# Values as weights in the attention's second product, with row sums from the exponential and heads that need no turning

## What is computed

```python
scores = einsum('bsghd,btgd->bghst', q, k) * scale
p = softmax(scores, axis=-1)
out = einsum('bghst,btgd->bsghd', p, v)
...
cat = concatenate([core, xout], axis=-1)
catq = div_clamp_fp8(cat, proj_smooth)       # a scale for each head feature
y = einsum('bsi,oi->bso', catq, wproj) * (proj_in_scale * proj_w_scale)
```

## Time and profile before

| | |
|---|---|
| median of 3 runs | 1736.24 us (1735.25 to 1736.79) |
| the profiled execution | 1738.57 us, its span 1736.7 us |
| TensorE | busy 1632.1 us, 94% of the span |
| VectorE | 1410.2 us, 81% |
| ScalarE | 1359.8 us, 78% |
| GpSimd | 1089.6 us, 63% |
| DMA queue of SyncE | 68.1% of 16 engines' span |
| mean granted TensorE clock | 0.992 |

### The profile page before, as it was taken

How to read it: one execution, slowest core, us unless ns; L and a number is a source line. 1 busy time by engine, 2 the same in 40 slices (tenths; PEclk the granted TensorE clock), 3 DMA queues, 4 the chain that set the end, 5 groups by cost and what they waited for, 6 DMA issues and landing times.

```text
span 1736.7 us, 43799 instructions
## 1 busy us (share of the span) xinstructions
PE 1632.1 (94%) x15491; PEld 1228.0 (71%) x15776; DVE 1410.2 (81%) x3228; ACT 1359.8 (78%) x2908; POOL 1089.6 (63%) x1031
## 2 busy tenths in 40 slices
PE   1569999999999999999999999999999899999999
PEld 1447778888888888888888888888888544444444
DVE  8999999999999999999999999998779763323232
ACT  6978999999999999999999999999999622222221
POOL 1357777777787777777777777778777613121211
PEclk9969999999999999999999999999999999999999
DMA  5947788887888888788878887888999980303000
GB/s 177 223 111 127 140 154 144 148 153 147 148 149 156 147 145 152 147 148 146 151 147 149 148 159 147 145 140 151 188 187 187 196 244 22 138 8 142 4 24 25
DMA packets 663603, 241.45 MB, mean 139 GB/s; under 512 B 619488, under 2 KB 636000, under 8 KB 662880
## 3 DMA queue, kind: packets, MB, share of 16 engines
q1 hardware_dynamic: 662096, 230.20, 68.1%
q0 software_dynamic: 1296, 8.52, 2.4%
HBM read 75.15 MB, written 29.51 MB: 60 GB/s over the span
## 4 chain that ended last, share of the span: by engine, by line
PE 71%; DVE 9%; ACT 7%; issue 5%; POOL 4%; SPq 3%; DMA 2%; DVEq 0%; ACTq 0%; POOLq 0%
PE ps_pj L673 21%; PE ps_s L739 6%; PE ps_o L722 5%; PE ps_o L724 5%; PE ps_o L723 5%; PE ps_s L742 5%; PE ps_s L680 4%; PE ps_qt L692 4%; POOL local L1131 2%; PE ps_s L738 2%; PE ps_pj L811 2%; PE ps_s L825 2%; PE ps_o L811 2%; PE ps_pj L812 2%; PE ps_o L812 2%
## 5 line engine op out<-in xcount | busy, mean ns | idle before, releaser
L1131 POOL TENSOR_TENSOR local<-local 128x512 bf16<-128x512 f32 x512 | 597.1, 1166 | 296.3 <-ACT local L1035 296.0
L673 PE MATMUL ps_pj<-wide 128*128 128x256 bf16 (+1 forms) x5544 | 582.7, 254 | 4.8 <-DVE wide L1214 4.0
L673 PEld LDWEIGHTS ps_pj<-wide 128*128 128x128 bf16 x5544 | 470.1, 98 | 115.0 <-DVE wide L1214 4.4
L1032 ACT ACTIVATE local<-ps_s,neg_max 128x512 f32<-128x512 f32 x512 | 391.8, 765 | 43.7 <-DVE neg_max L1429 41.6
L1035 ACT ACTIVATE local<-ps_s,neg_max 128x512 bf16<-128x512 f32 x512 | 394.0, 770 | 0.0
L722 PE MATMUL ps_o<-v_hi,local 128*128 128x129 bf16 x2048 | 375.5, 221 | 5.7 <-DVE local L1437 3.2
L724 PE MATMUL ps_o<-v_hi,local 128*128 128x129 bf16 x2048 | 375.2, 219 | 0.0
L723 PE MATMUL ps_o<-local 128*128 128x128 bf16 x2048 | 375.1, 218 | 0.0
L1429 DVE TENSOR_REDUCE neg_max<-ps_s 128x1 f32<-128x512 f32 x512 | 344.7, 673 | 22.8 <-PE ps_s L742 22.7
L941 ACT ACTIVATE local<-ps_pj,head_rstd 128x128 f32<-128x128 f32 x756 | 242.0, 448 | 41.8 <-issue 41.7
L1106 POOL TENSOR_TENSOR head_rstd<-sq_sum,minus_half 128x3 f32<-128x3 f32 x256 | 223.4, 873 | 16.4 <-DVE sq_sum L1321 16.4
(11 more groups left out here) (133 smaller groups left out, 2623.5 us busy)
## 6 DMA issues: line engine op xcount, KB each, us to landing
quantised_heads<-local SPq DMA_DIRECT2D x128, 128.0 KB, 2.4
w_raw<-w_group SPq DMA_DIRECT2D x56, 256.0 KB, 3.2
wide<-quantised_heads SPq DMA_DIRECT2D x3, 4096.0 KB, 13.1
local<-local SPq DMA_TRANSPOSE x640, 3.2
wide<-packed_weights SPq DMA_DIRECT2D x32, 256.0 KB, 3.2
wide<-x SPq DMA_DIRECT2D x6, 1024.0 KB, 12.0
packed_weights<-w_proj POOLq DMA_DIRECT2D x4, 1024.0 KB, 15.2
wide<-quantised_heads SPq DMA_DIRECT2D x16, 256.0 KB, 3.4
```

What stands on the lines that cost most here:

```text
L673: last = mm(dst[:, at:at + n], lhs, w_at(par, part, c, cross * 512 + at, n), start=(k == 0), stop=(k == len(terms) - 1))
L1032: a(p_exp[:, u % 2], ps_s[u % 2][:], ACT.Exp, bias=neg_max[:, u % 4:u % 4 + 1])
L1131: tt_(pp[:, u % PP_BUFS, 1], p_exp[:, u % 2], pp[:, u % PP_BUFS, 0], ALU.subtract)\
```

## The change

The value product is turned round: the values are the weights, and P, already transposed, is the moving operand. Two units are taken together, so that a matmul has 256 columns, and twelve matmuls serve two units, six of them at lag 5 of the pair's second unit and six at lag 6. The product comes out with features on partitions. So the heads need no DMA transpose, and a head's smoothing scale is a column, one number for a partition. The row sums no longer come from a column of ones: the first exponential of a unit (L1032) gives its row's sum as an accumulator output. Their reciprocal, 128x4 for a head, goes to DRAM and comes back broadcast to all partitions, 2 KB for each. One y step of 128x512 serves a head and stands in front of the quantiser, whose lags go from 6 and 9 to 8 and 11. ScalarE still writes the high part of the values. The transposes of P now wait for the pair that had the buffer.

```diff
-        PV_LAG, Y_LAG, HEAD_LAG, STORE_LAG = 5, 6, 10, 12
+        PV_LAG, STORE_LAG = 5, 12
+        SUM_LAG, SUM_OUT_LAG, SUM_IN_LAG = 2, 3, 5
-        QUANT_LAG, QUANT_END_LAG = 6, 9
+        QUANT_LAG, QUANT_END_LAG = 8, 11
...
-                            sp.wait_ge(pv_done, SLOTS * g + u - PT_BUFS + 1)
+                            sp.wait_ge(pv_done, SLOTS // 2 * g + (u - PT_BUFS) // 2 + 1)
...
-                    for H in head_at(slot, HEAD_LAG, first):
+                    for H in head_at(slot, SUM_OUT_LAG, first):
+                        n = GROUP_HEADS * g + H
+                        sp.wait_ge(rsum_done, n + 1)
+                        sp.dma_start(sums_dram[n].rearrange("(p t) -> p t", t=TT), r_inv[:, H % 2]).then_inc(sums_out[H % 2], 16)
+                    for H in head_at(slot, SUM_IN_LAG, first):
+                        n = GROUP_HEADS * g + H
+                        sp.wait_ge(sums_out[H % 2], 16 * (n // 2 + 1))
+                        sp.wait_ge(y_done, n - 1 + HEAD_FREE)
+                        sp.dma_start(inv_sums[:, H % 2], sums_dram[n].partition_broadcast(P)).then_inc(sums_in[H % 2], 16)
...
-                        sp.dma_start_transpose(heads_t[:, H % HEADS].rearrange("p (q s) -> p q s", s=P), heads_n[:, H % 2])\
-                            .then_inc(turned[H % 2], 16)
...
-                        sp.dma_start(dst, heads_t[:, h]).then_inc(heads_stored, 16)
+                        sp.dma_start(dst, heads_n[:, H % 2]).then_inc(heads_stored, 16)
...
+            def values(u, start, end):
+
+                b, cross = u // UNITS, u // TT % HEADS // HPG
+                at = (u - 1) % TT * P
+                acc = ps_o[u // TT % 2][:, at:at + 2 * P]
+                pair = slice((u - 1) % PT_BUFS, (u - 1) % PT_BUFS + 2)
+                for tc in range(start, end):
+                    vh, vl = v_hi[:, b % 2, cross, tc], v_lo[:, b % 2, cross, tc]
+                    ph, pl = pt[:, pair, tc], pt[:, pair, TT + tc]
+                    mm(acc, vh, ph, start=(tc == 0), stop=False)
+                    mm(acc, vl, ph, start=False, stop=False)
+                    last = mm(acc, vh, pl, start=False, stop=(tc == TT - 1))
+                return last
...
+                    for u in unit_at(slot, PV_LAG + 1, first):
+                        if u % 2 == 1:
+                            values(u, TT // 2, TT).then_inc(pv_done, 1)
                     for u in unit_at(slot, PV_LAG, first):
...
+                        if u % 2 == 1:
+                            for i in (u - 1, u):
+                                pe.wait_ge(pt_landed[i % PT_BUFS], 16 * SLOTS // PT_BUFS * g + 16 * (i // PT_BUFS + 1))
+                            pe.wait_ge(y_done, GROUP_HEADS * g + u // TT - 1 + HEAD_FREE)
+                            values(u, 0, TT // 2)
...
-                        a(p_exp[:, u % 2], ps_s[u % 2][:], ACT.Exp, bias=neg_max[:, u % 4:u % 4 + 1])
+                        a(p_exp[:, u % 2], ps_s[u % 2][:], ACT.Exp, bias=neg_max[:, u % 4:u % 4 + 1],
+                          accum_out=r_sum[:, H % 2, qt:qt + 1])
...
-                    for u in unit_at(slot, Y_LAG, first):
-                        dve.wait_ge(pv_done, SLOTS * g + u + 1)
-                        v.reciprocal(r_sum[:, u % 4:u % 4 + 1], ps_o[u % 2][:, D:D + 1]).then_inc(rsum_done, 1)
...
-                        v.scalar_tensor_tensor(y[:, H % 2, qt * D:(qt + 1) * D], ps_o[u % 2][:, 0:D],
...
+                    for H in head_at(slot, SUM_LAG, first):
...
+                        v.reciprocal(r_inv[:, H % 2], r_sum[:, H % 2]).then_inc(rsum_done, 1)
...
                     for H in head_at(slot, QUANT_LAG, first):
...
+                        dve.wait_ge(pv_done, 2 * (n + 1))
+                        dve.wait_ge(sums_in[H % 2], 16 * (n // 2 + 1))
+                        v.scalar_tensor_tensor(y[:, H % 2].rearrange("p (t q) -> p t q", q=P),
+                                               ps_o[H % 2].rearrange("p (t q) -> p t q", q=P), smooth_of(g, H),
+                                               inv_sums[:, H % 2].rearrange("p (q t) -> p t q", t=TT), ALU.mult, ALU.mult)\
+                            .then_inc(y_done, 1)
```

More of the change, by code:

```diff
@@ L280, in block_kernel @@
         rsum_done = sem("rsum_done")
+        sums_out = [sem(f"sums_out{i}") for i in range(2)]
+        sums_in = [sem(f"sums_in{i}") for i in range(2)]
         plo_done = sem("plo_done")
         pt_landed = [sem(f"pt_landed{i}") for i in range(PT_BUFS)]
-        turned = [sem(f"turned{i}") for i in range(2)]
         pv_done = sem("pv_done")
@@ L439, in quad_place, with smooth_of @@
             return (q // 2 + 1) % 2, q % 2
-        def smooth_rows_of(group_index, head):
-            return rsmooth[:, bass.ds((group_index % 2) * (HEADS * D) + head * D, D)]
+        def smooth_of(g, H):
+            at = (g + H // GROUP_HEADS) * HEADS + H % HEADS
+            return inv_smooth[:, at:at + 1]
         def tile_bank(i, t):
@@ L581, in group @@
                         load_next_heads(slot - NEXT_HEADS)
[L582 to L585, removed]
-                    for H in head_at(slot, HEAD_LAG, first):
-                        sp.wait_ge(heads_done, GROUP_HEADS * g + H + 1)
[L588 to L591, removed]
-                        sp.dma_start_transpose(heads_t[:, H % HEADS].rearrange("p (q s) -> p q s", s=P), heads_n[:, H % 2])\
-                            .then_inc(turned[H % 2], 16)
-                    for H in head_at(slot, STORE_LAG, first):
-                        sp.wait_ge(turned[H % 2], 16 * GROUP_HEADS // 2 * g + 16 * (H // 2 + 1))
+                    for H in head_at(slot, SUM_OUT_LAG, first):
[7 more added lines that the diff above has]
+                        sp.dma_start(inv_sums[:, H % 2], sums_dram[n].partition_broadcast(P)).then_inc(sums_in[H % 2], 16)
+                    for H in head_at(slot, STORE_LAG, first):
+                        sp.wait_ge(heads_done, GROUP_HEADS * g + H + 1)
                         sp.wait_ge(heads_stored, 16 * (GROUP_HEADS * g + H + FREE))
@@ L1031, in group @@
                             act.wait_ge(plo_done, SLOTS * g + u - 1)
-                        a(p_exp[:, u % 2], ps_s[u % 2][:], ACT.Exp, bias=neg_max[:, u % 4:u % 4 + 1])
+                        H, qt = u // TT, u % TT
+                        if qt == 0 and (not first or H >= 2):
+                            act.wait_ge(rsum_done, GROUP_HEADS * g + H - 1)
+                        a(p_exp[:, u % 2], ps_s[u % 2][:], ACT.Exp, bias=neg_max[:, u % 4:u % 4 + 1],
+                          accum_out=r_sum[:, H % 2, qt:qt + 1])
                         if not first or u >= PP_BUFS:
@@ L1155, in _ @@
             v.reciprocal(rscale, c_("in_scale", 0, SETS * CH)).then_inc(ones_set, 1)
-            v.reciprocal(inv_smooth[:], c_("smooth", 0, G * HEADS)).then_inc(smooth_inverted, 1)
+            v.reciprocal(inv_smooth[:], c_("smooth", 0, G * HEADS))
             v.tensor_tensor(pscale[:], c_("proj_in"), c_("proj_w"), ALU.mult)
@@ L1430, in group @@
                             .then_inc(max_done, 1)
[L1431 to L1440 removed]
+                    for H in head_at(slot, SUM_LAG, first):
+                        n = GROUP_HEADS * g + H
+                        dve.wait_ge(exp_done, TT * (n + 1))
+                        if n >= 2:
+                            dve.wait_ge(sums_out[H % 2], 16 * (n // 2))
+                        v.reciprocal(r_inv[:, H % 2], r_sum[:, H % 2]).then_inc(rsum_done, 1)
                     for n, at in enumerate(CTX_SLOTS if first else ()):
```

55 lines of the change are left out of this document (14 added, 41 removed).

## The result

The changed kernel takes 1887.15 us in the median of 4 runs (1886.15 to 1887.59), the kernel before 1735.74 us beside it (1733.53 to 1736.79): a ratio of 1.0874, 95% interval 1.086 to 1.0887, or 151 us. The forecast was 1749 us, with a range up to 1782. The profiled execution after has 1887.02 us and a span of 1885.2 us.

What follows compares the result with a forecast made beforehand. TensorE was taken to set the pace, VectorE and ScalarE about 5% behind. Terms -13.4 + 29 - 3 + 0 = +12.6 us, put on the timed median of 1736.2, gave 1749 us; 8-in-10 range 1718 to 1782.

Steps and rivals of the forecast that it cites:

- the place: VectorE: the quantiser's new slots meet weight preparation, delaying the maximum; 1.2 us per 16 slots, +29 us, bounds 0 to 72.
- The other three quarters: VectorE, heads without the weight cast: two slots' work sums to 4.83 us, not late, charged nothing.
- the forecast's own limit of 7.0 us: VectorE, cast's quarter, slots 2 and 3 modulo 4: below about 7.0 us the lateness is absorbed; 7.58 forecast.
- y, priced 0.60: VectorE's 128x512 y, priced as the quantiser's last step: 0.60 us, up to twice that for the strided read.
- The read-out, taken at 0.055 us: ScalarE, first exponential's row sum: an instruction's fixed part, 0.055 us a unit, upper bound 0.32.
- the slack that was to take it: ScalarE: 2.28 us needed a slot, averaged over eight, 0.20 us slack; 2.34 with the read-out against 2.46.
- Rival (b): ScalarE: dear read-out, slower from about 0.15 us; 1762 us at 0.20, 1816 at 0.32; chance 0.18.
- TensorE's 13.4 us: Value matmuls: twelve of 256 columns replace twenty-four, saving 0.026 us a slot, 13.4 us over 512 slots.
- Rival (a): TensorE's gain comes through because the late maximum is absorbed: 1722 us, 1712 to 1723 at best; chance 0.28.
- The queue, charged nothing: SyncE's queue and DMAs: moved traffic about equal, transpose landings hidden with 2.3 us left; charged nothing.
- Start and end, taken as -3: VectorE's relief in group 0, worth up to 10 us, taken as -3; after 1340 us 0, bounds -3 and +3.
- full pace in 1060 to 1340 us: Sign that the forecast is right: no slowdown in that stretch, where no weights are prepared.

Runs made afterwards that it cites:

- before_readout: The kernel before with only the first exponential's row sum added, into a tile that nobody reads; 1776.49 us, ratio 1.0239.
- prep_moved: The changed kernel with the weight preparation two slots later, except in the first group; 1791.12 us, ratio 1.0323.
- six_prep_moved: The changed kernel with six buffers for the turned P, y's sums read in order, and weight preparation two slots later; 1782.38 us, ratio 1.0271.
- no_readout: The changed kernel without the first exponential's row sum (sums set to 1 once); 1893.90 us, ratio 1.0911.
- six_bare: six_both without the row sums and without the sums' store and load; 1759.72 us, ratio 1.0139.
- six_both: The changed kernel with six buffers for the turned P, quantiser at lags 6 and 9, sums loaded a slot earlier and read in order; 1803.56 us, ratio 1.0392.
- y_contiguous: The changed kernel with y reading the broadcast sums in order instead of with a step of four elements; 1846.98 us, ratio 1.0637.
- six_swapped: six_both with y running over PSUM and its output in steps, so only the sums are read in order; 1998.82 us, ratio 1.152.
- turned_store: six_both with the sums stored turned, element by element, so y can read them in order; 2520.9 us, ratio 1.451.

## Why the prediction was wrong

The sum of the 151 us, step by step from the kernel before to the changed one: the read-out 41 (before_readout), the rest 15 (prep_moved less before_readout), the place 96 (changed kernel less prep_moved). These are differences along one path, and another order would share them out otherwise: the place's term holds what the strided y and the read-out make of the pile-up, and alone in the kernel before it is 48.

**The step that failed: "The other three quarters have lighter pieces; without any they are ... 4.83, not late, and I charge them nothing."** The mechanism was right and its sign named: VectorE late, maximum late, exponential late, TensorE idle before the scores. But each of the four heads in 16 slots meets a piece of the preparation, and a bare sum was used for three of them. Between the maximum that starts at 802.08 us and the one at 810.53 VectorE is busy 7.86 us (2 x 0.59 maximum, 0.60 end, 1.06 and 1.36 scale pieces, 0.67 tile, 1.17 y, 1.80 quantiser make 7.84) and idle 0.59. The same stretch of the cast's head is 8.03, for which the forecast had 7.58; of the head with the other scale pieces (to 844.26) 8.12; of the head with the weight sums (to 832.91) 6.81. Three heads of four are past the forecast's own limit of 7.0 us where it counted one, and even the fourth is late, after VectorE has waited 1.57 us there for ScalarE's squares. The weights are prepared in this way beside 96 heads (24 times 16 slots), so the 96 us are 1.0 a head, where 1.2 per 16 slots were charged, 0.3 a head. The place alone in the kernel before, 48 us, also lies above the 29. Had I charged each of the three heads by the forecast's own formula (the excess over the limit and 0.6), it would have come to some 75 us with y at 0.60 and to some 115 us with the measured y: estimates from the sums above, on both sides of the 96.

**y, priced 0.60**, takes 1.17 by the starts, just inside the upper bound of 1.2. Of the difference, 0.39 is the strided read (1.133 against 0.739), worth 40 us in the changed kernel (0.31 a head) and 9 us where the pile-up is gone (prep_moved to six_prep_moved, two buffers more included). VectorE's forecast relief of 0.64 us a head was so about 0.1.

**The read-out, taken at 0.055 us**, takes 0.09: inside the bounds and nearer the lower one. What failed is the slack that was to take it: "ScalarE then needs 2.34 us of a slot that TensorE would make 2.46". That is a mean over eight slots, and by the earlier trace rows seven of them were full before: with a turn 2 x 0.57 + 1.33 = 2.47, with a tile 1.14 + 1.28 = 2.42. The free time lay in the one slot with neither. With 0.09 the two kinds need 2.56 and 2.51 us; before_readout shows 2.55 and 2.52. That the slot without turn or tile can't win it back because the next norm waits for GpSimd (0.70 us at 819.17) fits these rows, but no run took that wait away. Rival (b) named this bound and put its start at 0.15 us; at 0.09 it was already passed, and cost more than the 29 us that (b) had for 0.20. That no_readout gained nothing fits a smaller limit hidden behind a larger one.

**TensorE's 13.4 us** were never seen in the time. The value matmuls of 256 columns do start 0.11 us apart (810.94, 811.05, 811.16 in the timeline), as forecast, but in no kernel did TensorE set the pace afterwards: even six_bare has 2.518 us a slot against 2.485. Rival (a), which lived on them, has a slip as well: 1736.2 less 13.4 and 3 is 1720, not 1722, which changes nothing in the argument. The 0.32 us a slot, an estimate with the 81 ns that the Trainium skill gives (TensorE: Matmul & The Clock Gate, Back-to-back issue gap), is not there either.

**The queue, charged nothing.** In the changed kernel this holds: TensorE's waits there are for ScalarE, not for transposes, and y never waits for the landing of the sums. It stops holding as soon as y stands at lag 6, where four buffers cost 55 to 65 us. The sums' store and load cost 16 us in six_both. The Trainium skill (DMA: Bandwidth & Descriptors, Specifications) speaks against pieces under 512 B; the 16 B rows were hidden in the changed kernel, and 4 B pieces, which no row of before could show, held the queue for up to 7.9 us and cost 717 us.

**Start and end, taken as -3.** Of the last 15 us about 7 are lost in the first group (69 exponentials have started by 299.3 us in prep_moved, 72 by 299.8 in before_readout), and the middle wins 2 back. Its weight preparation was not moved, and VectorE is busiest there. Another 6 come after 1098.8 us (132 slots of 2.611 us against 130 of 2.565), the last 3 behind the last exponential. The changed kernel has 67 by 299.2, the kernel before 73 by 298.3. The sign "full pace in 1060 to 1340 us" can't be read at these times, since the groups end later; where no weights are prepared, from 1379.7 to 1499.0 us, 47 exponentials take 2.59 us each, the pace with read-outs.

**Open**: why six_bare is still 25 us slower than the kernel before, why with the lags 6 and 9 the transposes of P come late, and what makes up the 15 us beyond their place in time. No kernel tried beats the kernel before; the fastest with the turned product that leaves nothing out is prep_moved.

## What to carry to other kernels

Sum a pipelined engine slot by slot, with the work that really stands in each slot, and compare each sum with the pace: both large errors here, VectorE's place and ScalarE's slack, came from a mean or a bare sum standing for unequal slots. To test what a moved step costs, move its neighbours and not the step, since taking the step back changes its waits for its inputs as well. An edit that gives nothing when removed from a slowed kernel may still cost 2.4% alone (the read-out): add it alone to the kernel before.

## What the runs showed of the hardware

- A 128x512 product of PSUM and SBUF operands on VectorE takes 0.739 us with the f32 operand in SBUF read in order (y_contiguous), 1.133 with a step of 4 elements there (the changed kernel), and 2.50 with SBUF in order but PSUM and the output in steps of 128 elements (six_swapped).
- ScalarE's row sum comes out by an instruction of its own, shown 0.19 to 0.51 us long and 0.09 us by the starts (before_readout); 512 of them cost 0.080 us each in a kernel whose ScalarE was nearly full.
- A busy share can stay full while the pace falls: in before_readout TensorE is busy 99% of 300 to 1060 us, at a full granted clock (1.00), with slots 3.7% longer than in the kernel before, where it is busy 751.60 of the same 760 us:

```profile
300.00:1060.00 760.00, 752.99 (x8106) 604.64 (x8104) 692.46 (x1677) 721.37 (x1844) 601.26 (x553) 1.00 0.78 143
```

- 512 pieces of 4 B a head (turned_store) held the queue 6.7 us in the mean and up to 7.9 in each of 33 waits between 500 and 1100 us, and cost 717 us against the same kernel with 128 pieces of 16 B (six_both, 1803.56 us).
